# A Mamba-like mixer with a bit-shifting Ffn on one core: the Ffn's integer stages for two image rows at once, the residual's scaling on ScalarE, and another table of stage times

## The reference

```
u  = layernorm(x);  xh, z = split(u @ W_in)              # 256 -> 512 + 512
xc = depthwise 3x3 convolution of xh
dt_r, B, C = split(xc @ W_xproj);  dt = softplus(dt_r @ W_dt + b_dt)
dtN = dt @ W_dtN + b_dtN
for each of the 2304 pixels:                             # a scan, h is (8, 512, 16)
    h = exp(dt * A) * h + (dtN * B) * xc;  y = sum(h * C) + Dskip * xc
x = x + (layernorm(y) * g + b) * silu(z) @ W_out + b_out
t = layernorm(x)                                         # of 256 channels
lo, hi, sa = first index with t > 0.5 in channels 32..47, 40..55, 48..63
val = lo + 16 * hi;  shl = (val << sa) & 255;  shr = val >> sa
res = shl where t[0], t[39] > 0.5, shr where t[0], t[40] > 0.5, else 0
add 2 at channel 64 + (res & 15) and at 72 + (res >> 4), where active
x = x + t + that                                         # the Ffn and its residual
```

## Time and profile before

| | us |
|---|---|
| median of 3 runs | 3854.43 |
| the runs | 3844.46 to 3861.37 |
| the profiled execution | 3850.34 |
| its span, first to last instruction | 3848.5 |
| mean granted clock of TensorE | 0.858 |

### The profile page before, as it was taken

How to read it: one execution, slowest core, us unless ns; L and a number is a source line. 1 busy time by engine, 2 the same in 40 slices (tenths; PEclk the granted TensorE clock), 3 DMA queues, 4 the chain that set the end, 5 groups by cost and what they waited for, 6 DMA issues and landing times.

```text
span 3848.5 us, 105654 instructions
## 1 busy us (share of the span) xinstructions
PE 3007.7 (78%) x34944; PEld 1624.3 (42%) x34944; DVE 3545.4 (92%) x12174; ACT 2946.9 (77%) x6050; POOL 3123.7 (81%) x5772
## 2 busy tenths in 40 slices
PE   4787888788778887888788878877887788778765
PEld 2344444444444444444444444444444444444332
DVE  2699999999999999999999999999999999999997
ACT  2678777887787778787888787778887888787764
POOL 0688888888888888888888888888888888888885
PEclk7788888888888998888799888988888889988877
DMA  2878887887788878887888778778887888788874
GB/s 60 214 196 216 223 212 201 215 226 205 206 214 220 210 209 211 216 215 209 210 223 215 207 209 223 207 205 208 221 218 205 214 212 222 205 213 217 211 189 105
DMA packets 397438, 790.44 MB, mean 205 GB/s; under 512 B 94553, under 2 KB 249178, under 8 KB 396890
## 3 DMA queue, kind: packets, MB, share of 16 engines
q1 hardware_dynamic: 396890, 783.68, 78.4%
HBM read 648.20 MB, written 96.73 MB: 194 GB/s over the span
## 4 chain that ended last, share of the span: by engine, by line
DVE 43%; ACT 22%; PE 17%; issue 8%; DMA 3%; POOL 3%; SPq 2%; ACTq 0%; POOLq 0%; DVEq 0%
DVE h L910 9%; DVE ps_a L894 7%; ACT ps_a L668 7%; DVE ps_a L897 6%; DVE h L913 6%; PE ps_s L615 4%; PE ps_y L510 3%; ACT ap L678 3%; PE ps_s L577 3%; DVE sz L966 2%; DVE res L1001 2%; ACT y L753 2%; ACT yn L803 2%; PE ps_y L494 2%; ACT xtok L703 2%
## 5 line engine op out<-in xcount | busy, mean ns | idle before, releaser
L668 ACT ACTIVATE ps_a<-dtb,a_n 128x384 f32<-128x384 f32 x2304 | 1252.8, 580 | 387.5 <-DVE h L913 375.7
L1181 POOL TENSOR_TENSOR h<-mp,up 128x128 f32<-128x128 f32 x2304 | 1056.6, 459 | 392.3 <-PE ps_y L510 171.1
L1171 POOL TENSOR_TENSOR mp<-ap,h 128x128 f32<-128x128 f32 x2304 | 1053.9, 457 | 111.3 <-ACT ap L678 0.8
L894 DVE TENSOR_TENSOR ps_a<-ps_a,h 128x192 f32<-128x192 f32 x2304 | 817.4, 355 | 162.1 <-ACT ps_a L668 158.6
L910 DVE SCALAR_TENSOR_TENSOR h<-xb,db,ps_a 128x192 f32<-128x192 f32 x2304 | 923.5, 401 | 7.3 <-PE ps_y L510 4.2
L913 DVE SCALAR_TENSOR_TENSOR h<-xb,db,ps_a 128x192 f32<-128x192 f32 x2304 | 929.7, 404 | 0.0
L510 PE MATMUL ps_y<-h,cw 64*32 64x256 f32 x18432 | 771.3, 453 | 126.1 <-POOL h L1181 75.8
L897 DVE TENSOR_TENSOR ps_a<-ps_a,h 128x192 f32<-128x192 f32 x2304 | 810.0, 352 | 0.0
L678 ACT ACTIVATE ap<-dtb,a_n 128x256 f32<-128x256 f32 x1152 | 521.6, 504 | 154.1 <-POOL h L1181 127.8
L1161 POOL TENSOR_TENSOR up<-xb,db 128x512 f32<-128x512 f32 x576 | 611.5, 1062 | 0.0
L510 PEld LDWEIGHTS ps_y<-h,cw 64*32 64x32 f32 x18432 | 317.1, 120 | 490.4 <-issue 244.0
(11 more groups left out here) (112 smaller groups left out, 4103.7 us busy)
## 6 DMA issues: line engine op xcount, KB each, us to landing
xb<-xd SPq DMA_DIRECT2D x576, 512.0 KB, 7.2
dtb<-xd SPq DMA_DIRECT2D x576, 512.0 KB, 7.0
xs<-xh SPq DMA_DIRECT2D x196, 192.0 KB, 3.6
xd<-dttok SPq DMA_DIRECT2D x288, 128.0 KB, 7.0
xin<-in_x_dram SPq DMA_DIRECT2D x144, 128.0 KB, 4.3
xd<-xtok SPq DMA_DIRECT2D x192, 96.0 KB
res<-in_x_dram SPq DMA_DIRECT2D x144, 128.0 KB, 5.8
out_dram<-res SPq DMA_DIRECT2D x144, 128.0 KB, 2.4
```

What stands on the lines that cost most here:

```text
L668: ins = act.activation(ps_a[buf][:, n, 0:2 * VD].rearrange("p (t d) -> p t d", t=2), dtb[:, u % DUNITS, 2 * buf:2 * buf + 2, 0:VD], ACT.Ex ...
L894: dve.tensor_tensor(a[:, 0], a[:, 0], last[:, 0], ALU.mult).then_inc(m0_done, 1)
L1171: pool.tensor_tensor(mp[:, G % 2], ap[:, Q % 2, G % 4], h[:, (G - 1) % HRING, :, VD:HALF], ALU.mult) \
L1181: pool.tensor_tensor(h[:, G % HRING, :, VD:HALF], mp[:, G % 2], up[:, Q % 2, G % 4], ALU.add) \
```

## The change

- The Ffn works on two rows at once, an odd one and the even one before it: the tiles have 2 * KT = 6 in place of KT = 3, and every part but `hot` has half as many instructions, each twice as large. `res` holds six tiles; they are stored together, six DMAs behind one wait.
- The scaling of the residual (L1001) moves from DVE to ACT (`scale_res`, one instruction for each of the six tiles, stage `res_scale`). ACT waits for `ffn` before the first, and `ffn_add_low` waits for `res_scaled`.
- The parts (now 13 and 4) all stand at place 1 of a step, several together in some steps, and spread from time 91 of the odd row (step 43 of the row after it) to time 108 (step 12 of the row after that).
- The table `AT` is new in most of its lines. Of all stages that move: one of the four `proj` parts goes from step 46 to step 2, `cw` from 42 to 45 and 28 to 33, `dt_add` from 14 and 19 to 10 and 16, `exp`/`log` from all at 13 to 8, 13 / 9, 15, the first `gate` from 20 to 17, `yt` one step ahead, `stack` from 3 to 27, `bounce` from 31 to 36, `store` from 7 to 12.
- `hots` shares `score`, and `taps` shares `y`, to make space.

```diff
-    "ffn": (96, 96, 97, 97, 98, 98, 99, 99, 100, 100, 101, 101, 102, 102, 103, 103), "dt_add": (-34, -29),
-    "cw": (-6, 13, 28), "gate": (68, 69, 70, 71), "store": (103,), "stack": (-141,), "load_res": (59,),
+    "ffn": (91, 91, 98, 99, 99, 99, 99, 100, 100, 101, 102, 102, 102, 103, 106, 106, 108), "dt_add": (-38, -32),
+    "cw": (-3, 13, 33), "gate": (65, 69, 70, 71), "store": (108,), "stack": (-117,), "load_res": (68,),
+    "bounce": (-12,), "states": (-5,), "load_xin": (-191,), "res_scale": (94, 95, 96, 99, 103, 103),
...
-            def store(r):
-                sp.wait_ge(final_ready, r + 1)
-                for k in range(KT):
-                    sp.dma_start(row_tokens(out, r, k), res[:, k, :]).then_inc(out_stored, SEM_DMA)
+            def store(pair):
+                sp.wait_ge(final_ready, pair + 1)
+                for n in range(2 * KT):
+                    sp.dma_start(row_tokens(out, 2 * pair + n // KT, n % KT), res[:, n, :]).then_inc(out_stored, SEM_DMA)
...
+            def scale_res(pair, k):
+                if k == 0:
+                    act.wait_ge(ffn, pair * FFN + 2)
+                act.activation(res[:, k, :], res[:, k, :], ACT.Identity, bias=sc2[:, k:k + 1], scale=sc1[:, k:k + 1]) \
+                   .then_inc(res_scaled, 1)
...
-                if n == 0:
-                    for k in range(KT):
-                        dve.tensor_scalar(hot[:, k, :], res[:, k, 0:64], mv2[:, k, 0:1], rs2[:, k:k + 1],
-                                          ALU.subtract, ALU.mult)
-                    dve.tensor_scalar(sc1[:], rs2[:], 1.0, None, ALU.add)
-                    ins = dve.tensor_tensor(sc2[:], rs2[:], mv2[:, :, 0], ALU.mult)
-                elif n == 1:
-                    for k in range(KT):
-                        dve.tensor_scalar(res[:, k, :], res[:, k, :], sc1[:, k:k + 1], sc2[:, k:k + 1],
-                                          ALU.mult, ALU.subtract)
+                if n < 2:
+                    if n == 0:
+                        dve.tensor_scalar(sc1[:], rs2[:], 1.0, None, ALU.add)
+                        dve.scalar_tensor_tensor(sc2[:], mv2[:, :, 0], -1.0, rs2[:], ALU.mult, ALU.mult)
+                    for k in range(3 * n, 3 * n + 3):
+                        ins = dve.tensor_scalar(hot[:, k, :], res[:, k, 0:64], mv2[:, k, 0:1], rs2[:, k:k + 1],
+                                                ALU.subtract, ALU.mult)
...
+                dve.wait_ge(res_scaled, pair * 2 * KT + 2 * KT)
...
                 for r, j in due("ffn", i, s):
-                    if j % 2 == place:
-                        ffn_part(r, j)
+                    if r % 2 == 1 and place == 1:
+                        ffn_part(r // 2, j)
```

More of the change, by code:

```diff
@@ L152, in build @@
         sz = sb("sz", [P, NG, TOK])
[L153 to L170, removed]
+        res = sb("res", [P, 2 * KT, DM])
+        st2 = sb("st2", [P, 2 * KT, 6])
+        mv2 = sb("mv2", [P, 2 * KT, 2])
+        rs2 = sb("rs2", [P, 2 * KT])
+        sc1 = sb("sc1", [P, 2 * KT])
+        sc2 = sb("sc2", [P, 2 * KT])
+        hot = sb("hot", [P, 2 * KT, 64])
+        score = sb("score", [P, 2 * KT, 3, 16])
+        best = sb("best", [P, 2 * KT, 3])
+        nib = sb("nib", [P, 2 * KT, 3], I32)
+        val = sb("val", [P, 2 * KT], I32)
+        shl = sb("shl", [P, 2 * KT], I32)
+        shr = sb("shr", [P, 2 * KT], I32)
+        dif = sb("dif", [P, 2 * KT])
+        resi = sb("resi", [P, 2 * KT], I32)
+        rnib = sb("rnib", [P, 2 * KT, 2], I32)
+        amp = sb("amp", [P, 2 * KT])
         ps_a = [ctx.enter_context(nc.psum_tensor(f"ps_a{n}", [P, 2, 512], F32)) for n in range(2)]
@@ L264, in build @@
         ffn = sem("ffn")
+        res_scaled = sem("res_scaled")
         marked = sem("marked")
@@ L455, in _ @@
                     for r, j in due("store", i, s):
-                        store(r)
+                        if r % 2 == 1:
+                            store(r // 2)
                     for r, j in due("stack", i, s):
@@ L867, in _ @@
                     for r, j in due("ln2_log", i, s):
-                        ln2_log_var(r)
+                        if r % 2 == 1:
+                            ln2_log_var(r // 2)
                     for r, j in due("ln2_scale", i, s):
-                        ln2_scale(r)
+                        if r % 2 == 1:
+                            ln2_scale(r // 2)
+                    for r, j in due("res_scale", i, s):
+                        if r % 2 == 1:
+                            scale_res(r // 2, j)
                     for r, j in due("ln1_scale", i, s):
@@ L878, in _ @@
                         copy_xh(r, j)
-        FFN = 12
         @block.vector
@@ L972, in add_residual @@
                 dve.wait_ge(out_done, r * KT + k + 1)
-                dve.tensor_tensor(res[:, k, :], res[:, k, :], shared_bank("out", r, k)[:, 0:DM], ALU.add) \
-                   .then_inc(res_added, 1)
+                part = res[:, r % 2 * KT + k, :]
+                dve.tensor_tensor(part, part, shared_bank("out", r, k)[:, 0:DM], ALU.add).then_inc(res_added, 1)
             def ln2_stats(r, k):
                 dve.wait_ge(res_added, r * KT + k + 1)
-                dve.bn_stats(st2[:, k, :], res[:, k, :]).then_inc(ln2_stat, 1)
+                dve.bn_stats(st2[:, r % 2 * KT + k, :], res[:, r % 2 * KT + k, :]).then_inc(ln2_stat, 1)
             def ln2_aggregate(r):
@@ L982, in ln2_aggregate, with ffn_stage @@
                 dve.memset(wait_pad2[:], 0.0)
[L983 removed]
+                for k in range(r % 2 * KT, r % 2 * KT + KT):
                     ins = dve.bn_aggr(mv2[:, k, :], st2[:, k, :])
                 ins.then_inc(ln2_var, 1)
[L987 removed]
+            def ffn_stage(pair, n):
                 if n == 0:
[L989 to L1002 removed]
+                    dve.wait_ge(ln2_rstd, pair + 1)
+                    dve.wait_ge(ln2_var, 2 * pair + 2)
+                else:
+                    dve.wait_ge(ffn, pair * FFN + n)
+                if n < 2:
[5 more added lines that the diff above has]
+                                                ALU.subtract, ALU.mult)
+                elif n == 2:
```

107 lines of the change are left out of this document (51 added, 56 removed).

## The result

The changed kernel takes 3887.0 us (median of four runs, 3884.5 to 3889.5) against 3854.4 for the kernel before (median of three; a fourth run took 8256 and is left out). The ratio is 1.0087, 95% interval [1.0058, 1.0116]: slower by 0.9%, a small loss but clear of noise, where 3709 was forecast.

The account below looks back on a forecast made before the run. DVE and POOL were taken to bound the kernel in turns, POOL alone after the change; its idle time falling from 5.07 to 2.0 us a row gains 147, span 3703, forecast 3709 us, range 3630 to 3800.

Parts of the forecast that it names:

- DVE's row: DVE's own work a row, forecast to fall from 74.0 to 70.4 us with the Ffn done for two rows.
- The bound of 11.4 a pair: Upper bound in us for DVE's two-row Ffn, forecast at 8.2, if chained parts each wait for one more POOL instruction.
- So POOL becomes the bound: With DVE at 70.4 us a row, POOL's own 71.9 was to set the row.
- The scaling on ACT: Three instructions a row of 0.61 us on ACT, 61.4 to 63.2, hidden if decays are in time; otherwise at most 1.8.
- The wait before step 8: POOL's wait there for PE's sum of steps 0 to 3, forecast at 1.5 us a row, between 1.1 and 2.4.
- the 2.8 that I gave to `xp` and the clock: PE's chain before step 8: 1.5 us less waiting for ACT's `xp`, and 1.3 if the clock stays up.
- the `proj` term: Two `proj` matmul groups come into PE's chain before step 8, adding half of 2.85, 1.4 us.
- All other places: POOL's waits for ACT elsewhere, at moved `gate`, `dt_add` and others: 0.5 us a row, between 0 and 3.4.
- The wait of `cw`: POOL's wait for the load of `cs`, 1.5 us a row, counted as gained with `cw` three steps back.
- POOL stands at the gate: Rival: POOL waits at step 17 for ACT's `yn`, idles 6.3 us a row, kernel slower at 3916; chance 0.04.

Follow-up runs that it names:

- e8: The new Ffn code under the old table, with 200 columns of a state on DVE and 56 on POOL instead of 192 and 64; 3841 us.
- e11: Changed kernel with `proj`, `xlnT`, `stack`, `bounce` back, y steps apart, scaling, Ffn tail and store later, and 200 columns on DVE instead of 192; 3842 us.
- e6: The changed kernel with the six scalings on ACT, the tail of the Ffn and the store later; 3983 us.
- e14: The kernel of e6 with `stack` and `bounce` back at steps 3 and 31; 3908 us.
- e1: The changed kernel with the times of `xlnT` and `proj` as before the change; 3830 us.
- e16: The changed kernel with `xlnT`, `proj`, `stack` and `bounce` all back at their old times; 3747 us.
- e17: The changed kernel with `stack` alone back at step 3, `bounce` left at step 36; 3819 us.
- e4: The changed kernel with `y_scale` at 56, `y_shift` at 58 and the first `y_stats` at 22; 3850 us.
- e13: The changed kernel with only `stack` and `bounce` back at steps 3 and 31; 3811 us.
- e18: The kernel of e16 with the y steps of e4 and the first `gate` two steps later, at 67; 3702 us.
- e3: The old Ffn code under the new table, except `ffn` and `store`, which stay as before; 3843 us.
- e2: The new Ffn code under the table of before, with only `ffn`, `store` and `res_scale` entries new; 3840 us.
- e15: The kernel of e2 with the first `cw` at -3 instead of -6 and nothing else moved; 3782 us.

## Why the prediction was wrong

**DVE's row: right.** 70.4 forecast, 77.72 - 7.43 = 70.3 measured. The price of clustering is seen in two rows of the changed kernel, which answer; DVE in the first, with POOL at rest, then DVE and POOL in the second:

```profile
2074.68 0.17 DVE L1025 TENSOR_SCALAR nib<-best 128x18 int32<-128x18 f32 x1
2074.77 0.16 DVE L1026 TENSOR_SCALAR amp<-amp 128x6 f32<-128x6 f32 x1
2074.97 0.18 DVE L1028 TENSOR_SCALAR nib<-nib 128x18 int32<-128x18 int32 x1
2075.05 0.16 DVE L1029 SCALAR_TENSOR_TENSOR amp<-hot,amp 128x6 f32<-128x6 f32 x1
2075.24 0.17 DVE L1031 SCALAR_TENSOR_TENSOR val<-nib 128x6 int32<-128x6 int32 x1
```

```profile
1607.01 0.18 DVE L1025 TENSOR_SCALAR nib<-best 128x18 int32<-128x18 f32 x1
1607.10 0.43 DVE L1026 TENSOR_SCALAR amp<-amp 128x6 f32<-128x6 f32 x1
1607.56 0.18 DVE L1028 TENSOR_SCALAR nib<-nib 128x18 int32<-128x18 int32 x1
1607.65 0.43 DVE L1029 SCALAR_TENSOR_TENSOR amp<-hot,amp 128x6 f32<-128x6 f32 x1
1608.11 0.17 DVE L1031 SCALAR_TENSOR_TENSOR val<-nib 128x6 int32<-128x6 int32 x1
```

```profile
1607.01 0.49 POOL L1186 TENSOR_TENSOR mp<-ap,h 128x128 f32<-128x128 f32 x1
1607.58 0.47 POOL L1196 TENSOR_TENSOR h<-mp,up 128x128 f32<-128x128 f32 x1
```

The same five instructions take 0.73 us from start to end alone, and 1.27 beside POOL, two of them 0.43 instead of 0.17. Over the 24 pairs they took 0.73 to 1.53, 1.11 in the mean, so 0.38 more than alone. The bound of 11.4 a pair had assumed 0.4 for each of eight chained parts; these five instructions are three such parts. The price comes, but at about a third of that, and the row stayed at 70.3.

**"So POOL becomes the bound": wrong as a mechanism.** POOL's own work was read correctly (71.8), but e8 takes 4.7 us a row from it and gains nothing, and e11 confirms it; DVE's 1.15 us more can hide a quarter of that, not the whole. What I did, to add POOL's waits to its work, was sound only as a sum; each wait had to be forecast from the engine at its other end.

**"The scaling on ACT", hidden: the price was right, the cover was not.** It is 82.5 us in all, and ACT stands 46.0 us before it for `hot`:

```profile
L784 ACT ACTIVATE res<-res,sc 128x256 f32<-128x256 f32 x144 | 82.5, 593 | 46.0 <-DVE hot L1013 46.0
```

This answers the earlier trace rows. ACT then copies `xh` late, and PE waits for it ahead of the convolution, 34.2 us in all, in nearly every turn from an even to an odd row (before, PE's waits there were 4.9 us). In e6 and e14 the same six instructions, moved some steps together with the end of the Ffn, cost 4 us a pair.

**"The wait before step 8": the step that failed first.** I took 1.5 us; 3.71 stand there. The chain on PE was to take 19.8 to 21.1 us from POOL's step 43 to the end of the sum of steps 0 to 3; it took 23.3. In the mean over rows 1 to 45, by the starts of PE's sums (us):

| PE's program | before | change | e1 | e16 |
|---|---|---|---|---|
| from sum 36-39 to sum 40-43 | 5.13 | 5.87 | 3.86 | 3.87 |
| from sum 40-43 to sum 44-47 | 7.15 | 9.80 | 7.49 | 7.72 |
| from sum 44-47 to the end of sum 0-3 | 13.54 | 11.25 | 11.26 | 10.92 |

The last stretch became 2.3 us shorter, close to the 2.8 that I gave to `xp` and the clock: PE idles 1.53 in it instead of 3.32, and its granted clock is 0.91 instead of 0.85. It is the `proj` term that was mis-sized: 1.4 for "two of the groups come in". Putting `xlnT` and `proj` back takes 2.0 and 2.3 us out of the first two stretches (e1), 4.3 together. One `proj` part more stands between sums 36 and 40, and the fourth among the convolutions, two parts where I priced one. I had them in the place "where PE had 0.84 to spare" and counted half of their old time. In the turn above they ran in part at the lower clock: the three took 5.83 us, where two took 2.85 before. They start late because the table puts them there; PE's waits for `xlnT` are 19.6 us in all. Not all of the 4.3 us reach the row: e1 gives 57 us back, 1.4 a row, and e16 brings the wait to 1.71.

**"All other places", 0.5: 2.2 came.** `cw` 0.54, the gate 0.52, ACT's `ap` 0.55, PE's sum before step 4 0.34, and small ones. Behind `cw` and `ap` stands the move that I did not price at all, put at nothing without a reason, and it is the second step that failed: `stack` from step 3 to 27. I looked at `bounce` and counted its steps; for `stack` I never asked which transfers its four would stand beside. It is worth 68 us (e17), the largest single entry. The wait of `cw` fell only by 0.97 of the forecast 1.5; with `stack` alone back (e17) it is gone but for the start. A third move is neither in the list of the change nor in the prediction: `y_scale` on ACT goes from step 55 to 57 and `y_shift` on DVE from 57 to 56, so DVE asks for `rsy` a step before ACT's place for it. Those are the 117 us at `nmy`; apart again, with `y_stats` two steps later, they give 37 us back (e4).

**The rivals.** "POOL stands at the gate", with 6.3 us idle and 3916, has the size (5.92, 3887) and not the mechanism: the gate is 0.52 of it, and in the turn above PE's sum before step 8 ran at 1.09 us, at full clock. My 4% for slower was too little for an argument in which the largest wait was taken near its lower end. That the time fell so near to this rival's 3916 is luck.

**The sum.** 3887 - 3709 = 178 us: 76 for `stack` and `bounce` (e13), 64 for `proj` on top of that (e16), 45 for y steps and gate (e18), 185 together. These are differences between whole kernels: they tell what each move cost here, not by what each term of the forecast missed.

**Open.** Why the new table is harmless to the old code (e3) and harmful to the new one was not isolated. With the old code ACT waits 101 us for `dtb`, with the new 165, and it has 82.5 us more to do. That the scalings turn a late load into a later decay is the likely link; the old code with `stack` back was not run, nor `cw` alone moved under the old code. How much of e18's gain the new Ffn code brings, and how much the table would bring without it, is open. So is what holds e18's row at 74 us: in its chain that ended last PE has 36%, ACT 23%, DVE 17% and POOL 11%, so no engine alone.

## What to carry to other kernels

An engine's work plus its idle time always gives the period; only an experiment that takes work away from it, and leaves the rest, tells whether it is the bound. When a plan of many stages is renewed, list every moved entry, and price each by what it will stand beside, on the DMA queue as on the engines. The entry without arithmetic (`stack`) cost 68 us here, while the Ffn's saved work by itself gained 10 (e2), and 68 with one `cw` entry moved (e15). Undo the entries one by one before the idea is judged: with four entries put back and four set anew, of some forty, the same code is 3.9% faster than the kernel before.

## What the runs showed of the hardware

The same 192 KB transfers landed in 3.6 us when issued at step 3, and in 7.2 when issued at step 27 beside the stores and loads of dt (3.5 in e13, which moves them back).

A three-element instruction on DVE lasted as long as POOL's addition beside it (changed kernel, DVE and then POOL):

```profile
2008.37 1.79 DVE L973 SCALAR_TENSOR_TENSOR nmy<-mvy,rsy 128x3 f32<-128x3 f32 x1 [2.48 <-ACT rsy L768]
```

```profile
2008.32 1.82 POOL L1216 TENSOR_TENSOR dt<-dt,dttok 128x768 f32<-128x768 f32 x1
```

It waited 2.48 us and then paid 1.6 more than the small instructions above. It started 0.05 us behind a long instruction of POOL and ended with it. This happened in 18 of the 48 rows (1.79 each time); in the other 30 it took 0.15 to 0.46. The Trainium skill, "SBUF — State Buffer", section "Who interferes with whom", has the rule: a VectorE instruction with two SBUF inputs, or in a two-port mode, and a GpSimd instruction that reads SBUF exclude each other, and whoever starts first holds the shared ports to its end. The trace agrees, here and in the cluster above. What a VectorE instruction pays by it depends on how much is left of POOL's neighbour: 0.26 beside a decay or addition of 0.47 to 0.49, 1.6 beside the addition of 1.82.
